# A vision tower's embedding stage in another order on all engines, with its halo gathered on GpSimd

## The reference, cut to what matters

```python
x_right = jnp.pad(x, ((0, 0), (0, 0), (0, 0), (1, 0)))[:, :, :, :-1]      # left, down, up alike
xc = jnp.concatenate((x, x_right, x_left, x_down, x_up), axis=1)
tokens = xc.reshape(B, C5, h, p, wgrid, p).transpose(0, 2, 4, 3, 5, 1).reshape(B, h * wgrid, p * p * C5)
normed = (tokens - mean) * jax.lax.rsqrt(var + LN_EPS) * ln_gamma + ln_beta
h = jnp.einsum('bnd,de->bne', normed, w) + b
h = h + attn(layernorm(h)); h = h + ffn(layernorm(h))                      # ffn: 8 experts, top 2
```

## Time and profile before

| | |
|---|---|
| median of 3 runs | 191.0 us (190.62 to 191.51) |
| the profiled execution's own time | 190.62 us |
| its span | 188.9 us, 3445 instructions |
| TensorE, ScalarE, VectorE, GpSimd busy | 170.3, 115.7, 140.1, 79.1 us |
| mean granted TensorE clock | 0.998 of full speed |
| moved by DMA | 18.38 MB |

### The profile page before, as it was taken

One profiled execution on the slowest core, in us unless ns is written; L12 is line 12 of the kernel. 1 busy time (PEld: TensorE's weight loads), 2 busy tenths in 40 slices (PEclk: granted clock), 3 DMA queues, 4 the chain that ended last, 5 costly groups with the idle time before them and its releaser, 6 DMA issues.

```text
span 188.9 us, 3445 instructions
## 1 busy us (share of the span) xinstructions
PE 170.3 (90%) x1129; PEld 147.9 (78%) x1129; DVE 140.1 (74%) x319; ACT 115.7 (61%) x206; POOL 79.1 (42%) x103
## 2 busy tenths in 40 slices
PE   0498879988989888899999999999999999999994
PEld 0386539968686667689999999899899899899994
DVE  5389894498764985698759868878788688788653
ACT  2399463543732463855795795796787786873730
POOL 7874000141299612960354354463562662660000
PEclk9999999999999999999999999999999999999999
DMA  5999999500001850018002702704604500000002
GB/s 122 221 307 308 243 223 243 120 0 2 20 25 52 309 140 3 0 18 251 24 3 68 221 2 89 204 0 125 167 0 135 157 2 0 0 3 0 0 0 83
DMA packets 14692, 18.38 MB, mean 97 GB/s; under 512 B 2436, under 2 KB 10745, under 8 KB 14679
## 3 DMA queue, kind: packets, MB, share of 16 engines
q1 hardware_dynamic: 14134, 18.19, 36.4%
q10 hardware_dynamic: 544, 0.03, 0.2%
HBM read 17.44 MB, written 0.39 MB: 94 GB/s over the span
## 4 chain that ended last, share of the span: by engine, by line
PE 61%; DVE 5%; POOL 3%; issue 1%; POOLq 0%; DVEq 0%
PE ps L371 29%; PE ps L1155 17%; PE ps L1157 8%; PE ps L1205 1%; PE ps L1204 1%; PE ps L1203 1%; DVE merge L1236 1%; PE ps L383 1%; DVE big_r L1236 1%; POOL h L571 1%; POOL halo L579 1%; DVE bn L1404 1%; PE ps L378 1%; POOL halo L584 1%; DVE shifted L1236 0%
## 5 line engine op out<-in xcount | busy, mean ns | idle before, releaser
L371 PE MATMUL ps<-big_r,wsplit 128*128 128x512 f32 (+1 forms) x245 | 61.5, 387 | 0.0
L771 ACT ACTIVATE early<-ps,b1t 128x512 f32<-128x512 f32 x48 | 32.8, 683 | 29.1 <-PE ps L371 27.3
L1155 PE MATMUL ps<-wsplit,big_r 128*128 128x384 f32 x168 | 49.7, 355 | 0.7 <-DVE big_r L1236 0.7
L1236 DVE TENSOR_TENSOR big_r<-early,big_r 128x512 fp32r<-128x512 f32 x48 | 35.9, 751 | 15.8 <-ACT big_r L333 15.4
L371 PEld LDWEIGHTS ps<-big_r,wsplit 128*128 128x128 f32 x245 | 41.9, 189 | 6.3
L1157 PE MATMUL ps<-wsplit,big_r 128*128 128x192 f32 x168 | 42.1, 251 | 0.0
L1155 PEld LDWEIGHTS ps<-wsplit,big_r 128*128 128x128 f32 x168 | 31.5, 188 | 2.7 <-issue 1.1
L1157 PEld LDWEIGHTS ps<-wsplit,big_r 128*128 128x128 f32 x168 | 32.0, 190 | 1.3
L333 ACT ACTIVATE big_r<-early 128x512 fp32r<-128x512 f32 x48 | 30.3, 632 | 1.5
L1576 DVE SCALAR_TENSOR_TENSOR merge<-sq,gates,merge 128x192 f32<-128x192 f32 x32 | 26.9, 865 | 0.0
L315 POOL TENSOR_TENSOR wsplit<-stage,wsplit 128x768 fp32r<-128x768 f32 x4 | 7.4, 1846 | 19.3 <-ACT wsplit L333 15.7
(11 more groups left out here) (240 smaller groups left out, 281.4 us busy)
## 6 DMA issues: line engine op xcount, KB each, us to landing
stage<-in_L_ffn_w SPq DMA_DIRECT2D x4, 576.0 KB, 6.6
early<-in_L_ffn_w SPq DMA_DIRECT2D x4, 576.0 KB, 5.9
shifted<-in_L_tok_w SPq DMA_DIRECT2D x6, 288.0 KB, 9.3
early<-in_x SPq DMA_DIRECT2D x3, 512.0 KB, 6.9
stage<-in_L_ffn_w SPq DMA_DIRECT2D x4, 384.0 KB, 3.9
stage<-in_L_ffn_w SPq DMA_DIRECT2D x8, 192.0 KB, 5.0
early<-in_L_ffn_w SPq DMA_DIRECT2D x4, 384.0 KB, 3.1
early<-in_L_ffn_w SPq DMA_DIRECT2D x8, 192.0 KB, 4.7
```

Of the source, the lines that this page charges most:

```text
L371: mm = nc.tensor.matmul(dst, lhs, rhs, start=(first and n == 0), stop=(last and n == 4))
L771: nc.scalar.activation(gf[:, j % NG], ps[:, HPB[j % 4], :], ACT.Gelu, bias=b1t[:, bass.ds(k, 1)]).then_inc(s_gelu, 1)
L1155: nc.tensor.matmul(ps[:, AB[t], 0:2 * D], g_hi[:, j % NG, tok], w2c, start=(f == 0), stop=False)
L1236: return nc.vector.tensor_tensor(o, a, b, op)
```

## The change

- The image is loaded in two parts per channel, six loads instead of three; a channel's users wait for both.
- `gather_halo` runs on GpSimd, after `neg_half` and before the masks, once all channels are there. It ran on VectorE between two pixel groups.
- TensorE begins with three products of the unit matrix with `band` (432 columns) into a bank that is zeroed later, and has a fourth between the first two channels' transposes. The products of gamma and beta stand before the third channel's transposes. Halo transposes wait for their half's three gathers, each in the bank of the pixel group of the same number.
- Chunks 0 and 1 come after 21 of the 30 beta products, the other nine behind them. The order of the chunks, of the merges, and of the high and low parts changes with it; the halo's come later.
- The load of `qkvb_row`, which nothing reads, is gone.

```diff
@@ -52,0 +53 @@
+    PARTS = 2
@@ -128 +128,0 @@
-        qkvb_row = sb("qkvb_row", [P, 3 * D])
@@ -255,2 +255 @@
-        HB = [1, 2, 7, 3]
-        HB_OF = [0, 1, None, 2]
+        HB = [1, 2, 3, 4]
@@ -270 +269 @@
-        MERGES += [(0, 2, 0), (0, 2, 1), (0, 2, 2), (0, 2, 3), "halo 0", (0, 2, 4), "halo 1"]
+        MERGES += [(0, 2, s) for s in range(SHIFTS)]
@@ -272 +271 @@
-        MERGES += [(1, 2, s) for s in range(1, SHIFTS)]
+        MERGES += ["halo 0", (1, 2, 1), "halo 1", (1, 2, 2), (1, 2, 3), (1, 2, 4)]
@@ -296 +295 @@
-            nc.vector.tensor_copy(halo_g[:, k, 1:GRID, 0:3 * QR].rearrange("p w (c q) -> p w c q", c=C),
+            nc.gpsimd.tensor_copy(halo_g[:, k, 1:GRID, 0:3 * QR].rearrange("p w (c q) -> p w c q", c=C),
@@ -298 +297 @@
-            nc.vector.tensor_copy(halo_g[:, k, 0:GRID - 1, 3 * QR:6 * QR].rearrange("p w (c q) -> p w c q", c=C),
+            nc.gpsimd.tensor_copy(halo_g[:, k, 0:GRID - 1, 3 * QR:6 * QR].rearrange("p w (c q) -> p w c q", c=C),
@@ -300 +299 @@
-            nc.vector.tensor_copy(halo_g[:, k, :, 64:HALO].rearrange("p w (c x) -> p w c x", c=C),
+            nc.gpsimd.tensor_copy(halo_g[:, k, :, 64:HALO].rearrange("p w (c x) -> p w c x", c=C),
@@ -354 +352,0 @@
-            sp.dma_start(qkvb_row[:], every(qkv_b)).then_inc(d_rows, 16)
@@ -406,2 +404,5 @@
-                sp.dma_start(early[:, c * QR * IMG:(c + 1) * QR * IMG],
-                             x[:, c].rearrange("b (r q) w -> r b (q w)", q=QR)).then_inc(d_img[c], 16)
+                for part in range(PARTS):
+                    rows = QR // PARTS
+                    sp.dma_start(early[:, (c * PARTS + part) * rows * IMG:(c * PARTS + part + 1) * rows * IMG],
+                                 x[:, c].rearrange("b (r p q) w -> p r b (q w)", p=PARTS, q=rows)[part])\
+                        .then_inc(d_img[c], 16)
@@ -500,0 +502,5 @@
+            pool.wait_ge(c_gath0, 1)
+            for c in range(C):
+                pool.wait_ge(d_img[c], 16 * PARTS)
+            gather_halo(0)
+            gather_halo(1)
@@ -655,6 +660,0 @@
-            act.wait_ge(c_ones, 3)
-            copy(wlmh[0:HALO, 2 * C:NX, D:D + 2],
-                 ones_f[0:HALO, 0:4].rearrange("p (k n) -> p k n", k=2)).then_inc(s_mw, 1)
-            act.wait_ge(s_hcopy, 8)
-            act.wait_ge(s_hedge, 2)
-            copy(xh[0:HALO, 2 * C:NX], x_halo[0:HALO]).then_inc(s_hhi, 1)
@@ -667,3 +667,2 @@
-            merged_high(0, 2)
-            act.wait_ge(s_merge, MERGES.index("halo 1") + 1)
-            copy(wlmh[0:HALO, 2 * C:NX, HIGH0:], wm_halo[0:HALO]).then_inc(s_whi, 1)
+            act.wait_ge(s_hcopy, 8)
+            act.wait_ge(s_hedge, 2)
@@ -670,0 +670,7 @@
+            merged_high(0, 2)
+            copy(xh[0:HALO, 2 * C:NX], x_halo[0:HALO]).then_inc(s_hhi, 1)
+            act.wait_ge(c_ones, 3)
+            copy(wlmh[0:HALO, 2 * C:NX, D:D + 2],
+                 ones_f[0:HALO, 0:4].rearrange("p (k n) -> p k n", k=2)).then_inc(s_mw, 1)
+            merged_high(1, 0)
+            merged_high(1, 1)
@@ -674,4 +679,0 @@
-            act.wait_ge(s_beta, 1)
-            copy(beta_part, ps[:, BETAB, 0:D]).then_inc(s_betapart, 1)
-            merged_high(1, 0)
-            merged_high(1, 1)
@@ -680 +682,2 @@
-            small_high(0)
+            act.wait_ge(s_merge, MERGES.index("halo 1") + 1)
+            copy(wlmh[0:HALO, 2 * C:NX, HIGH0:], wm_halo[0:HALO]).then_inc(s_whi, 1)
@@ -681,0 +685 @@
+            small_high(0)
@@ -682,0 +687,3 @@
+            act.wait_ge(s_beta, 1)
+            copy(beta_part, ps[:, BETAB, 0:D]).then_inc(s_betapart, 1)
+            small_high(2)
@@ -687 +693,0 @@
-            small_high(2)
@@ -798,2 +804 @@
-            for g in range(XGROUPS):
-                c, wh = g // 2, g % 2
+            def transposed_pixels(c):
@@ -801,5 +806,10 @@
-                for w in range(4):
-                    wx = 4 * wh + w
-                    mm = nc.tensor.transpose(ps[:, XB[g], w * P:(w + 1) * P],
-                                             tiles[c][:, wx].rearrange("p q x -> p (q x)"), ident)
-                mm.then_inc(s_xt, 1)
+                for wh in range(2):
+                    for w in range(4):
+                        mm = nc.tensor.transpose(ps[:, XB[2 * c + wh], w * P:(w + 1) * P],
+                                                 tiles[c][:, 4 * wh + w].rearrange("p q x -> p (q x)"), ident)
+                    mm.then_inc(s_xt, 1)
+            def warm(count):
+                for _ in range(count):
+                    nc.tensor.matmul(ps[:, BETAB, 0:432], ident, band[:, 0:432], start=True, stop=True)
@@ -806,0 +817,4 @@
+            warm(3)
+            transposed_pixels(0)
+            warm(1)
+            transposed_pixels(1)
@@ -819,0 +834 @@
+            transposed_pixels(2)
@@ -821 +835,0 @@
-            pe.wait_ge(s_gather, 2 * GATHERS)
@@ -824,3 +838,4 @@
-                if HB_OF[n] is not None:
-                    pe.wait_ge(s_xsq, HB_OF[n] + 1)
-                    pe.wait_ge(s_xlo, HB_OF[n] + 1)
+                if wh == 0:
+                    pe.wait_ge(s_gather, (k + 1) * GATHERS)
+                pe.wait_ge(s_xsq, n + 1)
+                pe.wait_ge(s_xlo, n + 1)
@@ -841 +856 @@
-            ORDER = (0, 1, 2, 6, 7, 3, 4, 5)
+            ORDER = (0, 1, 2, 3, 4, 6, 7, 5)
@@ -875,2 +890,2 @@
-            def beta_products(half):
-                for s in range(SHIFTS):
+            def beta_products(half, shifts=range(SHIFTS)):
+                for s in shifts:
@@ -881 +895,0 @@
-            pe.wait_ge(s_hcopy, 6)
@@ -885 +899,8 @@
-            beta_products(1)
+            beta_products(1, (0, 1))
+            def whole_chunk(ch):
+                pe.wait_ge(s_wlo, ORDER.index(ch) + 1 - (ORDER.index(ch) > 5))
+                for t in range(TT):
+                    mm = embed(ch, t)
+                    if ch == ORDER[-1] and t % 2:
+                        mm.then_inc(s_emb, 1)
@@ -887,0 +909,6 @@
+            pe.wait_ge(s_mw, 1)
+            pe.wait_ge(s_xhi, 4)
+            pe.wait_ge(s_xlo, 4)
+            whole_chunk(0)
+            whole_chunk(1)
+            beta_products(1, (2, 3, 4))
@@ -890,11 +917 @@
-            pe.wait_ge(s_mw, 2)
-            for ch in ORDER[0:C]:
-                pe.wait_ge(s_wlo, ch + 1)
-                for t in range(TT):
-                    embed(ch, t)
-            pe.wait_ge(s_gb, 2)
-            pe.wait_ge(d_halo_w, 16 * HALO_W_DMAS)
-            for k in range(2):
-                beta_product(gb_halo[0:HALO, k], w_halo[0:HALO, k])
-            pe.wait_ge(d_tokb, 16)
-            beta_product(band[0:1, BAND0 - 1:BAND0 + 1], tokb_row[:]).then_inc(s_beta, 1)
+            whole_chunk(2)
@@ -915,6 +932,3 @@
-            pe.wait_ge(s_wlo, C + 1)
-            pe.wait_ge(s_hhi, 1)
-            pe.wait_ge(s_hlo, 1)
-            for ch in (2 * C, 2 * C + 1):
-                for t in range(TT):
-                    embed(ch, t)
+            whole_chunk(3)
+            whole_chunk(4)
@@ -923,0 +938,14 @@
+            pe.wait_ge(s_sqpart, 1)
+            small_transposes(2)
+            pe.wait_ge(s_gb, 2)
+            pe.wait_ge(d_halo_w, 16 * HALO_W_DMAS)
+            for k in range(2):
+                beta_product(gb_halo[0:HALO, k], w_halo[0:HALO, k])
+            pe.wait_ge(d_tokb, 16)
+            beta_product(band[0:1, BAND0 - 1:BAND0 + 1], tokb_row[:]).then_inc(s_beta, 1)
+            pe.wait_ge(s_hhi, 1)
+            pe.wait_ge(s_hlo, 1)
+            pe.wait_ge(s_mw, 2)
+            whole_chunk(2 * C)
+            whole_chunk(2 * C + 1)
@@ -929,10 +956,0 @@
-            def last_chunk(c):
-                pe.wait_ge(s_wlo, C + 2 + c)
-                for t in range(TT):
-                    mm = embed(C + c, t)
-                    if c == C - 1 and t % 2:
-                        mm.then_inc(s_emb, 1)
-            last_chunk(0)
-            pe.wait_ge(s_sqpart, 1)
@@ -943,3 +961 @@
-            small_transposes(2)
-            last_chunk(1)
-            last_chunk(2)
+            whole_chunk(2 * C - 1)
@@ -1250 +1266 @@
-            dve.wait_ge(d_img[0], 16)
+            dve.wait_ge(d_img[0], 16 * PARTS)
@@ -1252 +1268 @@
-            dve.wait_ge(d_img[1], 16)
+            dve.wait_ge(d_img[1], 16 * PARTS)
@@ -1269 +1285 @@
-            dve.wait_ge(d_img[2], 16)
+            dve.wait_ge(d_img[2], 16 * PARTS)
@@ -1272,3 +1287,0 @@
-            dve.wait_ge(c_gath0, 1)
-            gather_halo(0)
-            gather_halo(1)
@@ -1276 +1288,0 @@
-            low_pixels(3)
@@ -1280,2 +1291,0 @@
-            low_pixels(4)
-            low_pixels(5)
@@ -1320,0 +1331,4 @@
+                if s == 0:
+                    low_pixels(3)
+            low_pixels(4)
+            low_weights(1, 0, w_sum[:, 0, 0], slice(0, P))
@@ -1321,0 +1336,4 @@
+            low_weights(2, 1, w_sum[:, 0, 1], slice(0, P))
+            merge(0, 2, 1)
+            low_pixels(5)
+            merge(0, 2, 2)
@@ -1326 +1344 @@
-            merge(0, 2, 1)
+            merge(0, 2, 3)
```

(26 more changed lines are left out.)

10 lines of the change are left out of this document (5 added, 5 removed).

## The result

The changed kernel takes **187.8 us** in the median of four runs (187.67 to 188.18), the kernel before 190.88 (190.62 to 191.51, four runs): ratio 0.9837, 95% interval 0.9808 to 0.9865. The forecast was 187.5, in a range of 186.2 to 189.3. The profiled execution took 188.18 us, with a span of 186.4 (190.62 and 188.9 before). So the total came out as forecast: the prediction's own sum, 3.2 us taken from the median of 191.0, gives 187.8. The pair of profiled executions differs by 2.44 us only. The experiments show that the parts did not come out: how the gain was shared out among the edits in the prediction is wrong. A ratio leaves out executions that took over 1.5% more than the fastest of their kernel.

A forecast was written before the change was run, and what follows sets the result against it. TensorE's embedding stage, its third chunk waiting for VectorE, was taken as the bound. 2.7 us for order plus 0.8 for image and clock, less 0.3 for port and tie, gave 3.2 us: 187.5 us forecast, range 186.2 to 189.3.

The forecast's parts named there:

- What bounds the kernel: Embedding stage on TensorE: the third chunk's start, held by VectorE's low weights, sets the stage's end, 12.9 us of work later.
- After the stage, the gain goes through whole: Behind the embedding stage: no wait on a load takes up the gain, so all of it reaches the total.
- The order on VectorE: VectorE's queue before the third chunk: six gathers leave, low parts spread between merges; third chunk at 22.1, 2.7 us less.
- copies end at 17.45: ScalarE's halo copies, taken to end as before; the low weights of chunk 0 then come at 17.9 to 18.0.
- merges begin at 13.2: VectorE after the third retile, two low parts, gamma copy, small sums and memsets: merges begin 3.4 us earlier.
- Image and clock together: Six image loads and idle products: earlier image, faster transposes, ScalarE's chain 0.9 earlier, third chunk at 21.3; 0.8 us more.
- The gathers: Six halo gathers on GpSimd: 2.8 to 3.8 us, taken as 3.2, with 1 us of cover before ScalarE's copies.
- The port: VectorE merges beside GpSimd's gathers, both reading SBUF, may hold each other up: 0.3 us lost.
- The unread copy: Dropping the 288 KB load ahead of the expert weights: worth nothing itself, keeps a wait of up to 0.7 us from opening.
- The tie at chunk 3: TensorE needs chunk 3's low weights 3.0 us later, VectorE needs 2.9 us; taken at 0 to 0.2.
- Gathers and merges hold each other up: Rival, GpSimd against VectorE: gathers with waits make 5.8 us; total 190.2, or 189.2 with earlier images; chance 0.15.
- GpSimd sets the stage's end: Slower rival: six gathers on GpSimd decide the stage's end from 7.2 us on, total there 191.6; chance 0.05.

## Why the prediction came out right, and where it was wrong

- **What bounds the kernel: right, with less room than thought.** In the change and its near variants the third chunk begins some 0.15 us after the end of VectorE's low weights, and the 12.9 us behind it stayed 12.9. But the prediction had TensorE ready at 21.5, 0.6 us before VectorE. The nine beta products took 1.14 us instead of 0.8 and the first embedding product came at 18.58 instead of 18.3, so TensorE was ready at the same time, and it is the bound once VectorE's queue is cut further. "After the stage, the gain goes through whole": right, 2.49 us at the stage's end and 2.44 us in the two executions' times.
- **The order on VectorE, 2.7 us: the step that failed.** The step was to hold by itself, and it took two things of TensorE as given: "copies end at 17.45" and "merges begin at 13.2". The second is the gamma copy without a wait for gamma's and beta's products. Without the idle products TensorE meets one of them at most: with these products ahead of the third transposes, as in the change, the merges begin at 14.09 and the halo copies end at 19.1 to 19.2; with them behind, the copies end at 17.38 and the merges begin at 14.64. The order with the gathers off VectorE but without idle products gives 0.5 us in the median of all executions and 1.5 by its ratio; the order alone 0.1. With the idle products both premises held (13.11 and 17.05).
- **Image and clock together, 0.8: wrongly sized, both ways.** The image landed 0.2 us earlier in the change's profile and 0.4 in the mean, instead of 1.0 to 1.2, though the packets were nearly as fast as taken (0.130 us against 0.125). The idle products give 1.1 to 2.2 us, as they are what makes the order's 2.7 possible. The two mistakes stood on opposite sides. That they nearly cancel, so that 3.2 stands against 2.4 to 3.1 measured, is luck.
- **The gathers, 2.8 to 3.8: right**, 3.06 us. The Trainium skill (GPSIMD Engine Reference, Performance pitfalls for Q7 kernels) has a read with a step over 8 bytes cost half as long again. Here the line through the copy of 128 elements (0.29) and that of 384 in runs (0.51) gives 0.32 for 168 elements, and those with a step took 0.47: the trace agrees. The estimate of 4.0 worked out from it in the prediction was too long, as the 3.2 it started from had some 0.4 for the plain copy and 0.8 for the one of 384.
- **The port, 0.3: right in size** (0.25 us at the end), not in place: the scaled copies were slowed, 0.97 to 1.04 us for two instead of 0.55, not the scaled adds, which stood behind the last gather. By the Trainium skill (SBUF — State Buffer, Who interferes with whom) the lock holds for a whole instruction of either; the one retile beside the first gather stayed at 0.69 while the gather took 0.91 instead of 0.47, which agrees with VectorE having held the port first.
- **The unread copy, 0: right. The tie at chunk 3: right**, 0 (chunk 3 follows the sums of squares without a wait).
- **Rivals.** "Gathers and merges hold each other up" and "GpSimd sets the stage's end" did not come about; nor did "the image gains its full rate". The rival that I had not written was the one that mattered: that the parts don't add, because at 1.2 GHz the new order makes TensorE the bound.

Each part alone is worth 0.1, 0.5 and 0.6 us by its ratio (order, idle products, gathers; all three with 1 at or inside the interval), together 1.3; the whole is 3.1 in the first measurement and 2.5 in its repeat. The intervals would allow each part more, 0.6, 1.2 and 1.3 us, so that the parts don't add is shown by the waits in the traces rather than by these times. Three queues (VectorE's, ScalarE's behind the third transposes, TensorE's at the lower level) ended within about 1 us of each other, and each edit relieves one of them. The old order with both the idle products and the gathers on GpSimd wasn't tried, so what the order is worth beside them is left open.

## What to carry to other kernels

When an edit moves work to the front of an engine's queue, cost that work at the clock which the trace shows at that place, and follow who waits for what it was moved past; a term that says "the other engine's end stays where it is" needs a row. Where several queues end close together, take each edit out of the whole and add each to the old kernel: the two give different answers, and only the pair tells which edits need each other. Compare trace readings from the event that starts the queue, not from the start of the span, when that event wanders by half a microsecond and more.

## What the runs showed of the hardware that I had not expected

- **The clock falls behind short waits, and only in some executions.** In the profiles of six kernels the granted clock was at 0.50 in a stretch of some 3 us between 40 and 48 us, and their rest is 151.8 to 152.0 us instead of 151.2: 0.5 to 0.8 us. Waits of the same 0.7 and 0.8 us stand in profiles whose clock stayed at 1.00, those of the kernel before and of the change among them. With two more idle products in each wait the mean clock was 0.999 or more in six executions of six. In the kernel before with idle products it was at 0.50 from 14 to 16 us, behind waits of 0.70 and 1.06 us, although the transposes had run at the full level at 7 us.
- **When it first rises depends on little.** Without idle products the halo transposes show it: 0.12 us each in the kernel before at 14 us, at the lower level throughout in the kernel without idle products (3.62 for 16), and 2.41 for 16, partly one and partly the other, with the order alone. The times of the kernel without idle products spread over 3.5 us, the change's over 0.5 to 0.8. With idle products the first eight transposes took 1.16 us in one profile of the change and 1.75 in the other. That the moment of the rise is the cause is argued from these profiles, not shown, since only one run of each has a trace.
- **Faster packets, little earlier landing.** The queue moved 264 GB/s instead of 225 at 5 to 9 us, yet the third retile began 0.2 us earlier only. Part of this shows in the trace's packets: before the last packet of the images ended (9.56 us, before 9.78), 105 packets of 2304 bytes, of the weights behind them, had begun, before 35. At 11 to 17 us the weights moved at 258 GB/s instead of 311, but that is not the six loads' doing: other kernels with six loads had up to 328 there. Why it differs is open.
